# Attention stack kernel: last norms on GpSimd, x-stage logits in pairs, two query windows in one matmul, and another order of work in the slots

## The chip, the cores and the metric

The kernel runs on one core of a Trainium2 chip. Its time is the device time in microseconds (us) of one execution of the whole program; of several runs the median is given. The core's engines run side by side, each in the order of its own instruction stream, and wait for each other through semaphores: PE (TensorE, matrix products, with PEld for its weight loads), DVE (VectorE), ACT (ScalarE), POOL (GpSimd) and SP, which issues the DMAs.

## The reference, cut to what matters

There are 16 sequences of 128 tokens of 128 numbers. First comes one cross-attention layer (the x stage), then six layers, each a local attention and a gated feed-forward.

```python
x = x + tanh(g_xattn[0]) * xattn(layernorm(x), ctx, ctx, fside, ...)   # 16 heads of 8; bias from clip(frac_k - frac_q, -0.2, 0.2)
x = x + tanh(g_ffn[0]) * ffn(layernorm(x), ...)
# ffn:
for i in range(6):
    x = attn_layer(shift_tokens(x), Wqkv[i], ...) + x      # 16 heads of 64
    x = ffn_layer(shift_tokens(x), ln_g[i], ...) + x
# attn_layer: q = l2norm(q) * qs; k = l2norm(k) * ksc; rotary; then windows of 32 queries:
#   queries of window w see the keys of windows w-1 and w, with a band mask, softmax, times v; out @ Wo
# ffn_layer: xn = (x - mean) / sqrt(var + 1e-5) * g + b; (a * gelu(gate)) @ W2 + b2
# shift_tokens: the last 64 features of a token are taken from the token before it
```

## The kernel before, in words

A tile is one sequence (T, with n its number in the layer and par its parity). All state `z` stays on the chip. The order on each engine is written out by hand, in functions named `slot` of the same shape on all engines, and `layer_slots` runs 16 of them a layer: slots 0, 1, 14 and 15 are written out, slots 2 to 13 are a loop over pairs. A slot for tile T carries three tiles at once: it does scores and softmax of T, the projection of T+1 (chunks 0 to 5, of which 0, 1, 3 and 5 are halves of q and k and 2 and 4 are v), and the end of T-1 and T-2 (attention output, residual, LayerNorm statistics).

For a q or k chunk PE projects into one of two banks (`project`, L455 to L457, three matmuls of 512 columns), ACT squares it (L816), DVE multiplies by the rotary tables (`times_cos`, `times_sin`, L1091), sums the squares (L1103) and clamps (L1108), ACT makes the inverse norm by log and exp (`norms`, L820 and L822), POOL adds (`add_rotated`, L1502) and scales (`scale_rotated`, L1509), PE transposes (`qk_transpose`, L465) and ACT copies out. A bank is projected into again only when DVE is done with it (semaphore `rotated`).

For half the heads (h is 0 or 1) of a tile, `scores` (L476) fills `s_ps`, DVE adds the band mask (L1115) and takes row maxima (L1122), POOL subtracts them (`center`, L1515), ACT takes exp, PE transposes, `values` (L506) multiplies by v, DVE inverts the sums and normalises (L1130, L1134), PE transposes the result into `y_ps` (`att_transpose`, L516) and `out_project` (L524) follows. `scores` and `values` are 32 small matmuls each: 4 head pairs, 2 heads of a pair on the upper and lower 64 rows of PE's array (r), 4 windows of 32 queries (w), each writing 32 partitions. Windows 0 and 1 take the same 64 keys (`keys_of`).

The LayerNorm of T-2 in a slot: `add_out` (L1347) adds the residual, PE shifts the second 64 features into `y_ps` (`shift_state`, L529), `ln_stats` on DVE multiplies the first 64 features of `z` by 1.0 into `xs` (L1352), copies the shifted ones from `y_ps` (L1353), and takes the statistics of the 128 (L1355); `ln_variance` (L1359), `ln_std` on ACT (L854, L856) and `ln_apply` on DVE (L1363, into `xn`) follow. `z_stage` (L1298) holds a tile of `z` for the next projection but one. PE's `att_transpose` for half 0 writes `y_ps` again and so waits for `xs_ready`, the mark that both parts of `xs` are there.

The x stage has slots of its own (`x_slot`): for each of four head groups g, `x_scores` on PE adds three matmuls of 512 columns for the bias (L565 to L567, all 128 rows) and one for the logits (L571, on 32 rows, those from 32g) in bank g % 2 of `s_ps`; DVE, ACT and POOL make probabilities, PE transposes (L485) and multiplies by the values (L581).

At a layer's end the feed-forward of the four groups of four tiles runs interleaved with the projection of the next layer's tile 0. There ACT holds the table for gelu, so `ln_std` of the last two tiles takes a table load before and after it (L1036, L1039), and the four `norms` of the next tile stand after the load L1053. POOL makes `f_lo` (`f_rest`, L1611), for which PE's `f_up` (L677 to L679) waits.

## Time and profile before

| | us |
|---|---|
| median of 3 runs | 2065.31 (2059.34 to 2075.24) |
| the profiled execution's own time | 2061.48 |
| its span, first to last instruction | 2059.7 |
| span up to the first scores of layer 1 (x stage and start) | 274.3 |
| one layer, from scores to scores | about 289 |
| a loop slot of a layer | 15.2 to 15.5 |
| a loop slot of the x stage | 13.3 |
| busy: PE, DVE, ACT, POOL | 1797.2, 1600.0, 1384.6, 1332.1 |

The profile is of one execution. The span leaves out 1.8 us of its own time. The granted clock of PE was 0.97 of full speed over the span and 1.00 in the loop slots shown below.

### The profile page before, as it was taken

To read this page: it belongs to the slowest core of one execution; us is meant where nothing else is said; L and a number is where in the kernel's file an instruction comes from. 1 tells how busy PE (TensorE), PEld (TensorE's weight loads), DVE (VectorE), ACT (ScalarE), POOL (GpSimd) and SP (SyncE) were. 2 spreads that over 40 slices of the span, in tenths; PEclk is the share of its full clock that TensorE was granted. 3 is DMA by queue.
4 is the path that set the end of the run, shared out by engine and by line. 5 is a ranking of instruction groups with operands and counts; after the bars stand their busy time and mean duration, and the time that the engine had idled before them with its cause. 6 is when DMAs were issued, how large, how long until landed. Compare 5 with 4: busy or idle time off the path is not lost.

```text
span 2059.7 us, 86637 instructions
## 1 busy us (share of the span) xinstructions
PE 1797.2 (87%) x33584; PEld 1401.8 (68%) x33584; DVE 1600.0 (78%) x3772; ACT 1384.6 (67%) x3701; POOL 1332.1 (65%) x1226
## 2 busy tenths in 40 slices
PE   6999878998879898789988899988898988899887
PEld 3445457777667776677776677776677776677766
DVE  5766679898468987488896589885689885689984
ACT  3677657777557776567775577775577775577765
POOL 3444467777467777377775477774677773677773
PEclk9999979999989999999999999999899999899999
DMA  5000021111021111111110211110211110211111
GB/s 121 4 5 5 1 70 33 35 37 32 25 64 41 31 36 28 63 34 33 40 31 23 68 40 31 41 31 23 64 44 31 31 42 22 65 37 37 31 33 46
DMA packets 59120, 77.81 MB, mean 38 GB/s; under 512 B 16608, under 2 KB 31674, under 8 KB 57914
## 3 DMA queue, kind: packets, MB, share of 16 engines
q1 hardware_dynamic: 58938, 75.36, 13.9%
q8 instruction: 117, 1.92, 0.4%
q14 instruction: 65, 0.53, 0.1%
HBM read 22.63 MB, written 1.05 MB: 11 GB/s over the span
## 4 chain that ended last, share of the span: by engine, by line
PE 60%; DVE 15%; issue 12%; ACT 6%; POOL 5%; SPq 0%; DMA 0%; DVEq 0%; ACTq 0%; POOLq 0%
PE proj_ps L455 7%; PE s_ps L476 7%; PE tr_ps L465 7%; PE y_ps L524 7%; PE proj_ps L457 5%; PE proj_ps L456 5%; PE y_ps L516 4%; DVE by_cos L1091 3%; PE pv_ps L506 3%; ACT square L816 3%; DVE by_sin L1091 3%; DVE xs L1352 3%; PE s_ps L571 3%; DVE sumsq L1103 2%; PE s_ps L691 2%
## 5 line engine op out<-in xcount | busy, mean ns | idle before, releaser
L1502 POOL TENSOR_TENSOR qk<-by_cos,by_sin 128x512 f32<-128x512 f32 x388 | 495.3, 1276 | 208.3 <-DVE by_sin L1091 201.9
L1509 POOL TENSOR_TENSOR qk<-qk,inv_norm 128x512 f32<-128x512 f32 x388 | 404.8, 1045 | 68.7 <-ACT inv_norm L822 41.6
L1091 DVE TENSOR_TENSOR by_cos<-proj_ps,tab 128x512 f32<-128x512 f32 x364 | 249.4, 685 | 159.6 <-ACT square L816 158.6
L816 ACT ACTIVATE square<-proj_ps 128x512 f32<-128x512 f32 x364 | 217.4, 597 | 195.1 <-PE proj_ps L457 194.8
L1515 POOL TENSOR_TENSOR s_sb<-s_sb,row_max 128x512 f32<-128x512 f32 x192 | 202.7, 1056 | 136.1 <-DVE row_max L1122 136.1
L455 PE MATMUL proj_ps<-w_hi,x_hi 128*128 128x512 f32 x546 | 273.8, 502 | 4.8 <-DVE by_sin L1091 2.6
L465 PE MATMUL tr_ps<-ident,qk 128*128 128x128 f32 x1544 | 247.2, 284 | 24.2 <-ACT x_hi L810 11.8
L1103 DVE TENSOR_REDUCE sumsq<-square 128x8 f32<-128x512 f32 x388 | 262.2, 676 | 0.0
L1091 DVE TENSOR_TENSOR by_sin<-proj_ps,tab 128x512 f32<-128x512 f32 x364 | 247.8, 681 | 0.0
L465 PEld LDWEIGHTS tr_ps<-ident,qk 128*128 128x128 f32 x1544 | 184.0, 146 | 72.5 <-POOL qk L1509 28.5
L457 PE MATMUL proj_ps<-w_hi,x_lo 128*128 128x512 f32 x546 | 222.1, 407 | 0.0
L456 PE MATMUL proj_ps<-w_lo,x_hi 128*128 128x512 f32 x546 | 221.6, 406 | 0.0
L516 PE MATMUL y_ps<-ident,att 128*128 128x128 f32 x768 | 117.8, 276 | 102.7 <-DVE xs L1353 102.7
L476 PE MATMUL s_ps<-k_T,q_T 64*32 64x64 f32 x12288 | 168.7, 227 | 36.8 <-issue 34.5
L524 PE MATMUL y_ps<-wo,att_T 128*128 128x128 f32 x1536 | 187.7, 275 | 0.0
L476 PEld LDWEIGHTS s_ps<-k_T,q_T 64*32 64x32 f32 x12288 | 137.2, 107 | 72.3 <-issue 72.3
L524 PEld LDWEIGHTS y_ps<-wo,att_T 128*128 128x128 f32 x1536 | 179.8, 192 | 8.7
L828 ACT ACTIVATE q_T<-tr_ps 128x512 f32<-128x512 f32 x193 | 114.9, 595 | 90.4 <-PE tr_ps L465 90.4
L516 PEld LDWEIGHTS y_ps<-ident,att 128*128 128x128 f32 x768 | 85.8, 141 | 116.3 <-issue 113.2
L506 PE MATMUL pv_ps<-arena,p_T 64*32 64x65 f32 x7680 | 163.7, 226 | 0.0
L506 PEld LDWEIGHTS pv_ps<-v,p_T 64*32 64x32 f32 x4608 | 122.0, 106 | 53.3 <-issue 52.8
L506 PE MATMUL pv_ps<-v,p_T 64*32 64x65 f32 x4608 | 153.3, 225 | 4.8 <-ACT p_T L846 4.8
(172 smaller groups left out, 4167.1 us busy)
## 6 DMA issues: line engine op xcount, KB each, us to landing
arena<-v SPq DMA_DIRECT2D x388, 130.0 KB, 2.4
w_raw<-in_L_ffn_Wqkv SPq DMA_DIRECT2D x7, 1536.0 KB, 7.3
wo<-in_L_ffn_Wo SPq DMA_DIRECT2D x7, 512.0 KB, 3.8
w_raw<-in_L_ffn_W SPq DMA_DIRECT2D x7, 341.0 KB, 5.5
c_in<-in_ctx SPq DMA_DIRECT2D x16, 64.0 KB, 1.8
xn<-in_fside_BxS SPq DMA_DIRECT2D x1, 1024.0 KB, 6.0
out<-z SPq DMA_DIRECT2D x4, 256.0 KB, 3.0
w<-in_L_ffn_W SPq DMA_DIRECT2D x12, 64.0 KB
```

Source lines behind the costliest of these rows:

```text
L455: pe.matmul(ps[:], x_hi[:], w_hi[:, col], start=True, stop=False)
L456: pe.matmul(ps[:], x_hi[:], w_lo[:, col], start=False, stop=False)
L457: pe.matmul(ps[:], x_lo[:], w_hi[:, col], start=False, stop=True).then_inc(proj_full, 1)
L465: mm = pe.transpose(tr_ps[:, 128 * j:128 * j + 128], qk[:, c, 128 * j:128 * j + 128], ident[:])
L476: mm = pe.matmul(s_ps[toks, slot_of(r, w), 64 * a:64 * a + 64], q_T[par][feat, PAIRS * h + a, toks], k_T[par][feat, PAIRS * h + a, keys_of ...
L506: mm = pe.matmul(pv2_ps[toks, r, (DH + 1) * a:(DH + 1) * (a + 1)], p_T[keys, h, a, toks], src[keys, PAIRS * h + a, :], start=True, stop=True)
L516: mm = pe.transpose(y_ps[:, 128 * j:128 * j + 128], att[:, 8 * i + 2 * j:8 * i + 2 * j + 2, :].rearrange("p a b -> p (a b)"), ident[:])
L524: mm = pe.matmul(y_ps[:, 0:D], att_T[:, c, :], wo[:, c, :], start=(c == 0), stop=(c == 7))
L1091: return dve.tensor_tensor(dst[:, c % 2, :].rearrange("p (h d) -> p h d", d=DH), ps, tb, ALU.mult)
L1103: dve.tensor_reduce(sumsq[:, c, :, 0], square[:, c % 2, :].rearrange("p (h d) -> p h d", d=DH), AX, ALU.add).then_inc(summed, 1)
L1502: pool.tensor_tensor(heads(qk[:, c, :]), heads(by_cos[:, c % 2, :]), heads(by_sin[:, c % 2, :])[:, :, ::-1, :], ALU.add).then_inc(qk_added, 1)
L1509: pool.tensor_tensor(ap, ap, inv_norm[:, c, :].unsqueeze(2).to_broadcast([128, 8, DH]), ALU.mult).then_inc(qk_ready, 1)
```

## The change

Six edits, in the core of the diff below.

1. `QUERIES`: in `scores` and `values` the first two windows become one matmul of 64 queries, so 24 matmuls stand where 32 stood, 8 of them of 64 queries and 16 of 32.
2. `ln_stats` no longer copies the first half of `z` into `xs`; statistics are taken of `z` and `xs` apart (two instructions of 64 numbers), and `ln_apply` has two instructions of 64 columns.
3. The orders in `slot` on PE, ACT, DVE and POOL change. On DVE `ln_apply` moves from after group 3 to before it, `z_stage` from before the mask of half 1 to after it, and the row maxima of half 1 come after two products; on PE `shift_state` comes after `project` 1 and `qk_transpose` 3, `att_transpose` 0 after `project` 2.
4. In the x stage `x_scores` handles two head groups: bias of g, logits of g, logits of g+1, bias of g+1.
5. At a layer's end POOL makes the last two deviations (`own_deviations`) and the four inverse norms of the next tile (`own_norm`) by power -0.5; ACT's `ln_std` there and one table load are gone, and one load of the exp table is left.
6. POOL's `scale_rotated` of a chunk at the layer's end follows directly on its `add_rotated`.

```diff
+QUERIES = [(slice(0, 2 * WINDOW), 1), (slice(2 * WINDOW, 3 * WINDOW), 2), (slice(3 * WINDOW, 4 * WINDOW), 3)]
...
@@ PE, scores (values likewise)
-                        for w in range(NT // WINDOW):
-                            feat, toks = slice(64 * r, 64 * r + 64), slice(WINDOW * w, WINDOW * w + WINDOW)
+                        for toks, w in QUERIES:
+                            feat = slice(64 * r, 64 * r + 64)
                             mm = pe.matmul(s_ps[toks, slot_of(r, w), 64 * a:64 * a + 64], q_T[par][feat, PAIRS * h + a, toks],
...
@@ PE, x stage
+            def x_bias(T, par, g, first):
+                hi, lo = flat(pos_hi[:, GH * g:GH * g + GH]), pos_lo[g]
+                pe.matmul(s_ps[:, g % 2, :], d_hi[:, par], hi, start=first, stop=False)
+                pe.matmul(s_ps[:, g % 2, :], d_hi[:, par], lo, start=False, stop=False)
+                return pe.matmul(s_ps[:, g % 2, :], d_lo[:, par], hi, start=False, stop=not first)
+
+            def x_logits(T, par, g, first):
+                rows = slice(32 * g, 32 * g + 32)
+                return pe.matmul(s_ps[:, g % 2, :], xq[rows, par, :], flat(xk_bd[rows, par]), start=first, stop=not first)
...
                 if after(T, 1) or g >= 2:
                     pe.wait_ge(masked, T * 4 + (g - 1))
+                x_bias(T, par, g, True)
                 if g == 0:
                     pe.wait_ge(xk_ready, T + 1)
+                if after(T, 1) or g >= 2:
+                    pe.wait_ge(masked, T * 4 + g)
+                x_logits(T, par, g, False).then_inc(s_full, 1)
+                x_logits(T, par, g + 1, True)
+                x_bias(T, par, g + 1, False).then_inc(s_full, 1)
...
@@ PE, x_slot
-                x_scores(T, par, 1)
...
-                x_scores(T, par, 3)
...
@@ ACT, a layer's end
-                act.preload_act_table_set("natural_log_exp_and_others")
-                ln_std(T - 2, 0)
-                ln_std(T - 1, 1)
-                act.preload_act_table_set("gelu_and_others")
+                act.sem_inc(log_done, 2)
...
@@ DVE
                 def ln_stats(T, n, par):
-                    zt = tile_of(z, n, 0, D // 2)
                     dve.wait_ge(sh_full, T + 1)
-                    dve.tensor_scalar(xs[:, par, 0:D // 2], zt, 1.0, None, ALU.mult).then_inc(xs_ready, 1)
-                    dve.tensor_copy(xs[:, par, D // 2:D], y_ps[:, 0:D // 2]).then_inc(xs_ready, 1)
-                    dve.wait_ge(xs_ready, T * 2 + 2)
-                    dve.bn_stats(stats[:, par], xs[:, par]).then_inc(stat_done, 1)
+                    dve.tensor_copy(xs[:, par], y_ps[:, 0:D // 2]).then_inc(xs_ready, 1)
+                    dve.bn_stats(stats[:, par, 0], tile_of(z, n, 0, D // 2))
+                    dve.wait_ge(xs_ready, T + 1)
+                    dve.bn_stats(stats[:, par, 1], xs[:, par]).then_inc(stat_done, 1)
...
                 def ln_apply(T, n, par):
                     dve.wait_ge(rstd_ready, T + 1)
-                    dve.tensor_scalar(tile_of(xn, n), xs[:, par],
-                                      mean_var[:, par, 0:1], rstd[:, par:par + 1], ALU.subtract, ALU.mult).then_inc(xn_ready, 1)
+                    for lo, src in ((0, tile_of(z, n, 0, D // 2)), (D // 2, xs[:, par])):
+                        last = dve.tensor_scalar(tile_of(xn, n, lo, lo + D // 2), src,
+                                                 mean_var[:, par, 0:1], rstd[:, par:par + 1], ALU.subtract, ALU.mult)
+                    last.then_inc(xn_ready, 1)
...
@@ POOL
+            def own_norm(T, c):
+                pool.wait_ge(norm_ready, T * 4 + (c + 1))
+                pool.tensor_tensor(inv_norm[:, c, :], sumsq_min[:, c, :], minus_half[:], ALU.pow).then_inc(inv_ready, 1)
...
+                def own_deviations(T):
+                    pool.wait_ge(var_ready, T)
+                    pool.tensor_tensor(log_var[:], mean_var[:, :, 1], eps[:].to_broadcast([128, 2]), ALU.add).then_inc(var_added, 1)
+                    pool.wait_ge(var_added, L)
+                    pool.tensor_tensor(rstd[:], log_var[:], minus_half[:, 0:2], ALU.pow).then_inc(rstd_ready, 2)
...
                 split_x(T)
+                own_deviations(T)
                 f_rest(2)
                 add_rotated(T, 0)
                 f_rest(3)
+                own_norm(T, 0)
+                scale_rotated(T, 0)
                 for c in range(1, 4):
                     add_rotated(T, c)
-                first_scales(T)
+                    own_norm(T, c)
+                    scale_rotated(T, c)
+                split_x(T + 1)
```

**PE at the start of a loop slot.** `s_ps<-k_T,q_T` is `scores`, and the size at the end is the output's: partitions by columns. Before:

```order
L470 ISA
L476 MATMUL s_ps<-k_T,q_T 32x64 x32
L445 REGISTER_ALU
L446 ISA
L455 MATMUL proj_ps<-w_hi,x_hi 128x512
L456 MATMUL proj_ps<-w_lo,x_hi 128x512
L457 MATMUL proj_ps<-w_hi,x_lo 128x512
L489 ISA
L490 REGISTER_ALU
L492 MATMUL pv_ps<-ident,p_sb 128x128 x4
```

Now:

```order
L481 MATMUL s_ps<-k_T,q_T 64x64
L481 MATMUL s_ps<-k_T,q_T 32x64 x2
L481 MATMUL s_ps<-k_T,q_T 64x64
L481 MATMUL s_ps<-k_T,q_T 32x64 x2
L450 REGISTER_ALU
L451 ISA
L460 MATMUL proj_ps<-w_hi,x_hi 128x512
L461 MATMUL proj_ps<-w_lo,x_hi 128x512
L462 MATMUL proj_ps<-w_hi,x_lo 128x512
L494 ISA
L495 REGISTER_ALU
L497 MATMUL pv_ps<-ident,p_sb 128x128 x4
```

The 32 equal matmuls became eight times a matmul of 64 queries and two of 32 (the last two of the eight are shown). In `values` it is the same.

**DVE in the second half of a loop slot.** `xn` is the LayerNorm of T-2, `by_cos` to `sumsq_min` the chunks of T+1. Before:

```order
L1103 TENSOR_REDUCE sumsq<-square 128x8
L1108 TENSOR_REDUCE sumsq_min<-sumsq 128x8
L1094 REGISTER_ALU
L1091 TENSOR_TENSOR by_cos<-proj_ps,tab 128x512
L1091 TENSOR_TENSOR by_sin<-proj_ps,tab 128x512
L1103 TENSOR_REDUCE sumsq<-square 128x8
L1130 RECIPROCAL inv_sum<-pv_ps 128x8
L1108 TENSOR_REDUCE sumsq_min<-sumsq 128x8
L1134 TENSOR_TENSOR att<-pv_ps,inv_sum 128x2x4x64
L1363 REGISTER_ALU
L1363 TENSOR_SCALAR xn<-xs,mean_var,rstd 128x128
```

Now:

```order
L1093 TENSOR_TENSOR by_cos<-proj_ps,tab 128x512
L1093 TENSOR_TENSOR by_sin<-proj_ps,tab 128x512
L1124 TENSOR_REDUCE row_max<-s_sb 128x8
L1105 TENSOR_REDUCE sumsq<-square 128x8
L1299 REGISTER_ALU
L1300 ISA
L1300 TENSOR_SCALAR z_stage<-z 128x128
L1110 TENSOR_REDUCE sumsq_min<-sumsq 128x8
L1364 REGISTER_ALU
L1364 TENSOR_SCALAR xn<-z,mean_var,rstd 128x64
L1364 ISA
L1364 TENSOR_SCALAR xn<-xs,mean_var,rstd 128x64
```

`xn` moved from the slot's end to between groups 2 and 3 and is in two parts, and `z_stage` now stands two instructions ahead of it. On POOL the order beside this place is now `add_rotated` 2, `center` 1, `scale_rotated` 2.

**PE in the x stage, one pair of head groups.** `pos_hi` and `f_hi` are the bias, `gelu,xq` the logits. Before:

```order
L565 MATMUL s_ps<-pos_hi,w_hi 128x512
L566 MATMUL s_ps<-f_hi,w_hi 128x512
L567 MATMUL s_ps<-pos_hi,w_lo 128x512
L571 MATMUL s_ps<-gelu,xq 128x512
L481 ISA
L483 REGISTER_ALU
L485 MATMUL pv_ps<-ident,p_sb 128x128 x4
L541 ISA
L542 REGISTER_ALU
L543 MATMUL tr_ps<-ident,arena 128x128
L544 MATMUL tr_ps<-ident,c_in 128x128
L581 MATMUL pv_ps<-p_T,arena 32x128 x4
```

Now:

```order
L578 ISA
L563 MATMUL s_ps<-pos_hi,w_hi 128x512
L564 MATMUL s_ps<-f_hi,w_hi 128x512
L565 MATMUL s_ps<-pos_hi,w_lo 128x512
L569 MATMUL s_ps<-gelu,xq 128x512 x2
L563 MATMUL s_ps<-pos_hi,w_hi 128x512
L564 MATMUL s_ps<-f_hi,w_hi 128x512
L565 MATMUL s_ps<-pos_hi,w_lo 128x512
```

The logits of two groups now follow each other, and the transposes and values that stood between groups g and g+1 come after both.

## Rows read from the trace of the kernel before

**Rows 1.** The page: busy time of the engines, its chain by engine.

```profile
PE 1797.2 (87%) x33584; PEld 1401.8 (68%) x33584; DVE 1600.0 (78%) x3772; ACT 1384.6 (67%) x3701; POOL 1332.1 (65%) x1226
...
PE 60%; DVE 15%; issue 12%; ACT 6%; POOL 5%; SPq 0%; DMA 0%; DVEq 0%; ACTq 0%; POOLq 0%
```

**Rows 2.** Three loop slots, the first and their mean: length, busy us of each engine.

```profile
666.32:681.55 15.23, 13.89 (x333) 11.58 (x341) 13.57 (x31) 11.18 (x30) 11.61 (x12) 1.00 0.14 34
...
sum 45.92, PE 41.74 PEld 34.71 DVE 40.93 ACT 33.88 POOL 35.18; mean PE 13.91 PEld 11.57 DVE 13.64 ACT 11.29 POOL 11.73
```

**Rows 3.** Waits: who waited for whom, us in total, times, longest.

```profile
PE y_ps L516 <- DVE xs L1353: 102.7, 78, 1.4
```

**Rows 4.** The chain in order of time in a loop slot: start, us, what.

```profile
701.60 0.76 DVE xs L1352
```

**Rows 5.** Timeline of a loop slot: start, us, engine, instruction [idle before, releaser].

```profile
685.65 1.27 POOL L1502 TENSOR_TENSOR qk<-by_cos,by_sin 128x512 f32<-128x512 f32 x1 [0.23 <-DVE by_sin L1091]
...
686.21 0.77 DVE L1352 TENSOR_SCALAR xs<-z 128x64 f32 x1
...
686.89 0.21 DVE L1353 COPY xs<-y_ps 128x64 f32<-128x64 f32 x1
...
687.14 0.29 DVE L1355 BATCH_NORM_STATS2 stats<-xs 128x6 f32<-128x128 f32 x1
...
687.25 0.63 PE L516 MATMUL y_ps<-ident,att 128*128 128x128 f32 x4 [1.34 <-DVE xs L1353]
```

**Rows 6.** Single lines: duration ns least/median/most, first and last start.

```profile
L1352 DVE TENSOR_SCALAR xs<-z x96: 143/762/768, 310.5 to 2025.5; 128x64 f32 x72, 128x64 f32<-128x64 f32 x24
...
L1363 DVE TENSOR_SCALAR xn<-xs,mean_var,rstd x96: 335/339/1210, 322.0 to 2031.1; 128x128 f32 x72, 128x128 f32<-128x128 f32 x24
...
L1298 DVE TENSOR_SCALAR z_stage<-z x98: 191/195/730, 251.2 to 2044.7; 128x128 f32 x72, 128x128 f32<-128x128 f32 x26
```

**Rows 7.** Timeline of that slot's second half.

```profile
692.16 0.68 DVE L1091 TENSOR_TENSOR by_sin<-proj_ps,tab 128x512 f32<-128x512 f32 x1
...
693.00 1.28 POOL L1502 TENSOR_TENSOR qk<-by_cos,by_sin 128x512 f32<-128x512 f32 x1 [0.23 <-DVE by_sin L1091]
...
695.12 0.69 DVE L1091 TENSOR_TENSOR by_cos<-proj_ps,tab 128x512 f32<-128x512 f32 x1 [1.49 <-ACT square L816]
```

**Rows 8.** Timeline at the start of a call of scores.

```profile
704.33 0.70 PEld L476 LDWEIGHTS s_ps<-k_T,q_T 64*32 64x32 f32 x64 [0.17 <-issue]
704.33 0.86 PE L476 MATMUL s_ps<-k_T,q_T 64*32 64x64 f32 x64
```

**Rows 9.** An x-stage loop slot: window as in rows 2, PE's timeline.

```profile
114.53:127.84 13.31, 12.75 (x78) 6.58 (x79) 8.80 (x35) 9.87 (x40) 5.23 (x7) 1.00 0.02 5
...
121.19 0.50 PE L565 MATMUL s_ps<-pos_hi,w_hi 128*128 128x512 f32 x1
...
121.53 0.39 PE L566 MATMUL s_ps<-f_lo,w_hi 128*128 128x512 f32 x1
...
121.76 0.40 PE L567 MATMUL s_ps<-pos_hi,w_lo 128*128 128x512 f32 x1
...
122.08 1.12 PE L571 MATMUL s_ps<-gelu,xq 32*128 32x512 f32 x2
...
123.14 0.66 PE L485 MATMUL pv_ps<-ident,p_sb 128*128 128x128 f32 x4
```

**Rows 10.** Timeline of a layer's end.

```profile
839.31 0.45 POOL L1496 TENSOR_TENSOR x_lo<-x_all,x_hi 128x128 fp32r<-128x128 f32 x1 [9.15 <-ACT x_hi L810]
...
840.79 1.27 POOL L1611 TENSOR_TENSOR f_lo<-f_all,f_hi 128x512 fp32r<-128x512 f32 x1 [1.02 <-ACT f_hi L963]
...
842.19 0.50 PE L677 MATMUL proj_ps<-f_hi,w_hi 128*128 128x512 f32 x1 [0.89 <-POOL f_lo L1611]
```

**Rows 11.** Groups by line: busy us, mean ns of one, idle before.

```profile
L1515 POOL TENSOR_TENSOR s_sb<-s_sb,row_max 128x512 f32<-128x512 f32 x192 | 202.7, 1056 | 136.1 <-DVE row_max L1122 136.1
...
L1496 POOL TENSOR_TENSOR x_lo<-x_all,x_hi 128x128 fp32r<-128x128 f32 x98 | 44.7, 456 | 92.4 <-ACT x_hi L810 92.2
```

More of the change, by code:

```diff
@@ L501, in values @@
                     for r in range(2):
-                        for w in range(NT // WINDOW):
-                            i, toks = slot_of(r, w), slice(WINDOW * w, WINDOW * w + WINDOW)
+                        for toks, w in QUERIES:
+                            i = slot_of(r, w)
                             keys = slice(64 * i, 64 * i + 64)
@@ L599, in x_slot @@
                     x_values(T - 1, 1 - par, 1)
-                x_scores(T, par, 1)
-                if not first:
                     x_p_transpose(T - 1, 3)
@@ L705, in slot @@
                         p_transpose(T - 1, 1)
-                    if behind >= 2:
-                        shift_state(T - 2, tile_of(z, n - 2, D // 2))
+                    if front_on:
+                        project(T + 1, 1)
                     if first:
@@ L731, in slot @@
                         qk_transpose(T + 1, 1)
+                        project(T + 1, 5)
                     values(T, par, 0)
-                    if front_on:
-                        project(T + 1, 5)
-                        if not last_front:
-                            x_transpose(T + 2)
+                    if front_on and not last_front:
+                        x_transpose(T + 2)
                     if behind >= 1:
@@ L928, in first_out @@
             def first_out(T):
-                for c in range(4):
-                    norms(T, c)
+                act.sem_inc(inv_log, 4)
                 x_out(T + 1)
@@ L1395, in slot @@
                         add_out(T - 2, n - 2)
-                    step(T, 0, behind, front_on)
-                    if behind >= 2:
-                        ln_stats(T - 2, n - 2, par)
+                    mask(T, 0)
+                    row_maxima(T, 0)
                     if not front_on:
@@ L1403, in slot @@
+                    if behind >= 1:
+                        sums_inverse(T - 1, 1)
+                    if behind >= 2:
+                        dve.wait_ge(stat_done, T - 1)
+                    if behind >= 1:
+                        normalise(T - 1, 1)
                     if behind >= 2:
                         ln_variance(T - 2, par)
+                    if front_on:
+                        clamp_norm(T + 1, 1)
+                    mask(T, 1)
+                    if not front_on:
+                        w_round(1, L + 1)
@@ L1590, in slot @@
                         pool.tensor_tensor(w1_lo[:], w1_raw[:], w1_hi[:].bitcast(f32), ALU.subtract).then_inc(w1_split, 1)
-                    for g in range(NG):
-                        if g == 0:
-                            if not first:
-                                scale_rotated(T, 3)
-                        elif front_on:
-                            scale_rotated(T + 1, g - 1)
-                        if g % 2 == 0:
-                            center(T, g // 2)
-                        if not front_on and 1 <= g < 3:
-                            w_rest(g - 1, L * 3 + g)
-                        if front_on:
-                            if g == 3 and not last_front:
-                                split_x(T + 2)
-                            add_rotated(T + 1, g)
-                layer_slots(pool.Fori, L, slot)
+                    if not first:
+                        scale_rotated(T, 3)
+                    center(T, 0)
+                    if not front_on:
+                        w_rest(0, L * 3 + 1)
+                    if front_on:
+                        add_rotated(T + 1, 0)
+                        scale_rotated(T + 1, 0)
+                        add_rotated(T + 1, 1)
+                        scale_rotated(T + 1, 1)
+                        add_rotated(T + 1, 2)
+                    center(T, 1)
+                    if not front_on:
+                        w_rest(1, L * 3 + 2)
+                    if front_on:
+                        scale_rotated(T + 1, 2)
+                    if front_on and not last_front:
+                        split_x(T + 2)
+                    if front_on:
+                        add_rotated(T + 1, 3)
+                layer_slots(pool.Fori, L, slot)
+                def own_deviations(T):
[3 more added lines that the diff above has]
+                    pool.tensor_tensor(rstd[:], log_var[:], minus_half[:, 0:2], ALU.pow).then_inc(rstd_ready, 2)
                 def f_rest(j):
```

129 lines of the change are left out of this document (63 added, 66 removed).

## Prediction

> **What bounds the kernel now.** I read the page first, then the windows of the loop slots, then the waits, the chain and the timeline. The page gives PE 87% of the span and 60% of the chain, DVE 78% and 15% [rows 1]. A share over the whole span doesn't say what an edit is worth, so I take the loop slot of a layer, which makes up most of the time. Three such slots are 45.92 us together, 15.31 us each; PE is busy for 13.91 us of a slot, DVE for 13.64, POOL for 11.73, ACT for 11.29 [rows 2]. PE's missing 1.4 us is nearly one wait: att_transpose waits for DVE's xs, 102.7 us over 78 slots, 1.32 us each [rows 3]. The chain confirms that it is on the path: it leaves PE, goes over DVE's products and sums to xs at L1352, and comes back to PE [rows 4]. The timeline shows what this step is: L1352 takes 0.77 us there and ends at 686.98, just after POOL's addition has ended at 686.92 [rows 5]. Its least duration is 143 ns, its median 762 [rows 6]. So about 0.6 us of it is a wait for POOL's instruction, and in that form the same can hit L1363 (335 ns least, 1210 most) and z_stage (191, 730) [rows 6]. DVE is nearly as full as PE: beside small gaps it idles 1.49 us in a slot, once, before the cosine product of group 3 [rows 7].
>
> The Trainium skill, page SBUF — State Buffer, section Who interferes with whom, has the shared port pair of VectorE and GpSimd as an exclusive lock, held for a whole instruction by whichever started first. By that rule, the trace agrees: 0.77 us against 0.14 [rows 5, 6].
>
> **The loop slots, part by part.** PE: with the wait gone a slot can't be shorter than PE's own work, about 13.9 us. The merged windows take a quarter of the matmuls out of four calls. A call is about 0.8 us (704.33 to 705.12 in the chain, 0.86 with the modelled end [rows 8]); the bounds are no gain, if the time goes by columns streamed per row and column of the array, and a quarter of it, 0.2 us, if it goes by instructions, so 0 to 0.8 us a slot. I take 0.2, since POOL and DVE will hide what goes beyond that, and keep the bounds for the range.
>
> DVE: from 13.64 us the xs instruction goes, at most 0.76, of which the copy after it overlapped a little: minus 0.70 [rows 4, 5]. One more statistics instruction of 64 numbers costs up to the 0.29 of the present one of 128 [rows 5]: plus 0.2. The xn instruction of 128 columns takes 0.34 [rows 6]; two halves cost the fixed part twice: plus 0.2. That gives 13.35 us, if nothing waits for POOL.
>
> But three of these DVE instructions now stand where POOL is busy. Before, add_rotated 2 started 0.84 us after the start of its sine product (692.16 to 693.00) and took 1.28, so it ended 2.1 us after that start [rows 7]. In the new order DVE does sine product 2, row maxima, sum of squares 2 and then z_stage, at three times 0.6 us = 1.8 us after the sine product's start. It meets the addition and waits 0.3 us. The clamp follows, and xn would start some 0.2 us later, at 2.3. POOL's next is center 1, whose row maxima have long been there; it starts about 0.1 us after the addition's end, at 2.2, and takes 1.06 [rows 11]. So the first half of xn comes 0.1 us too late and waits about 0.9 us. The second half then races scale_rotated 2; I let it win. DVE's slot is 13.35 + 0.3 + 0.9 = 14.55 us. PE needs 13.7, POOL and ACT less, and the wait for square 3 is covered by DVE's own lateness. I take 14.5 us: 0.8 us less than 15.3. Over the 78 slots that show the wait this is 62 us. For the 18 others, which begin or end a layer, I take nothing, for want of a steady pace.
>
> The other moves of order on PE, ACT and POOL cost nothing in this sum: their cover is the slack of PE, 14.5 against 13.7. Were DVE quicker, they would count, since PE's project 2 then waits for the sine product of group 0, which ends about when PE gets there.
>
> **The x stage.** PE is busy 12.75 of 13.31 us of a slot, so it is the bound [rows 9]. A group takes 1.95 us (121.19 to 123.14): bias to 122.08, logits 1.06 [rows 9]. Among equal shapes a matmul of 512 columns follows at 0.23 us (121.53, 121.76), but the logits, on 32 rows, start 0.32 us after the last bias [rows 9]: a change of shape has a price of about 0.1 us, and twice a pair is one change saved. If the logits of two groups, on different 32 rows, overlap as the 64-row halves of scores do (64 records in 0.86 us where one lasts over 0.2 [rows 8]), a pair saves the 1.06 of one and some of the changes, 1.3 us, so 2.6 a slot. PE would drop to about 10.5, and DVE (8.80 busy) and ACT (9.87 busy) [rows 9] are next; and the pair's second logits must wait for the mask of the group before. I take 2.0 us a slot, 14 slots, 28 us. If nothing overlaps, only the changes are saved, 0.4 us a slot, 6 us.
>
> **The layer's end.** Two table loads and four small ACT instructions leave ACT, and POOL gets ten small ones. PE is the bound there, working through the feed-forward; what can touch it is POOL's f_lo, for which PE waited 0.89 us [rows 10]. Before this f_lo POOL was idle 1.02 us [rows 10], and there own_deviations now stands, two instructions with a wait between. No row shows a power on POOL. The cheapest POOL row is 0.456 us for 128 columns, against 1.06 for 512 [rows 11], so 8 numbers should be nearer 0.3: two fit into 1.02. Were each 1.3 us, as long as a whole addition, PE would wait 1.8 us more, 11 us over six layers. A gain is bounded by the 0.89 us wait times six, 5 us. The inverse norms lie in POOL's long idle stretches. I take 0.
>
> **The sum.** The profiled execution took 2061.48 us, of which the span is 2059.7. 2061.5 - 62 - 28 = 1971.5. The median of the runs shown is 3.8 us above this execution; I give **1972 us**.
>
> **The rivals.** First, slower: the array drains. In scores and values, matmuls for 64 and for 32 queries now alternate, 16 changes a call. Where the shape changes today, PE's weight loads stand idle 0.17 us, though nothing was late [rows 8], and in the x stage too the follow-on is late [rows 9]. At 0.17 us a change a call gets 16 x 0.17 = 2.7 us longer, and 96 tiles x 4 calls = 384 calls make 1045 us: 1972 + 1045, about 3015 us. It decides from 90 / 384 = 0.23 us a call on, that is with two changes of sixteen that drain. For it: every change of shape in the trace shows the wait. Against it: in all of those the new shape takes rows and columns that the old one occupies, whereas here 64 queries write partitions 0 to 63 and the others 64 to 127, always the same parts, so nothing needs to be cleared.
>
> The Trainium skill, page TensorEngine Tiling (Array Packing), section Key Properties, states this rival's rule: changing the tiling mode, not just the tile, drains the TensorE. Its page TensorE: Matmul & The Clock Gate, section Part 3, has the position carried by each instruction, with tiles overlapping, which speaks for the forecast. No row here has two disjoint shapes in turn.
>
> Second, the port race is lost twice: the second half of xn finds scale_rotated 2 running, plus 1.05 us a slot. The slot is 15.5 us, the loop slots gain nothing, and only the x stage is left: about 2035 us, or 2025 if DVE's lateness shifts POOL a little. DVE's whole idle time of 1.5 us is then used up.
>
> Third, the race is won and the merging pays in full: DVE 13.4, PE 13.9 - 0.8 = 13.1, a slot of about 13.6. That is 1.7 x 78 = 133 and 28 off: about 1900 us.
>
> Fourth, the change doesn't do what it says in the x stage, no overlap of logits: the forecast plus 22, 1994 us.
>
> **How the numbers follow.** Forecast 0.35, and with the fourth case (0.09) in its surroundings 1940 to 2000; second case 0.22; third 0.15; drain 0.17; 0.02 for other mishaps above 2060. Leaving out the drain and the mishaps is 0.19, so the range goes from 1895 (third case) to 2045 (second with its spread). No change here means within 1%, 20.7 us, about what a measurement can tell. Faster: 0.35 + 0.09 + 0.15 + most of the second = 0.78. Same 0.05. Slower 0.17.
>
> **What the profile after would show.** Right: the wait of att_transpose for xs gone; loop slots of about 14.5 us with DVE busy over 14; xn's first half with a median near 1.2 us, its second near 0.3; z_stage near 0.5. A call of scores between 0.6 and 0.85 us; if over 1, the array drains. x slots of 11.3 us. POOL's powers under 0.5 us. I would be wrong mostly by the alternating shapes, whose price no row shows, and by the race for the port, where 0.1 us decides about 1 us a slot.

## The result and the profile after

| | before | after |
|---|---|---|
| median | 2064.48 us (2059.34 to 2075.24) | 3461.26 us (3455.89 to 3464.95) |
| ratio | | 1.675, 95% interval 1.668 to 1.682 |
| span of the profiled execution | 2059.7 us | 3460.0 us |
| granted clock of PE over the span | 0.97 | 0.85 |
| loop slot of a layer, mean | 15.3 us | 30.0 us |
| a call of scores | 0.8 us | 3.9 us |

The forecast was 1972 us. The rival that the array drains, with 3015 us and a chance of 0.17, is what happened, and it too was priced low. One of the four executions of w4_sin, a kernel below, took 2663 us at a granted clock of 0.56; its interval leaves it out.

The page of the kernel after: busy time, the granted clock in tenths by slices, the chain by engine, and one of the costliest groups (`s_sb<-s_ps` is the first step of DVE behind `scores`).

```profile
PE 3319.4 (96%) x27440; PEld 2425.7 (70%) x27440; DVE 1666.7 (48%) x3869; ACT 1376.0 (40%) x3617; POOL 1364.7 (39%) x1262
...
PEclk9987888877888888898888888888888887888888
...
PE 83%; issue 10%; POOL 3%; DVE 2%; ACT 1%; SPq 0%; DMA 0%; POOLq 0%; DVEq 0%; ACTq 0%
...
L1117 DVE TENSOR_TENSOR s_sb<-s_ps,band 128x512 f32<-128x512 f32 x192 | 132.8, 692 | 925.0 <-PE s_ps L481 925.0
```

DVE, ACT and POOL do the work of before in nearly the same busy time [rows 1]; PE's went from 1797 to 3319 us with 6144 records fewer. DVE now waits for `scores` 192 times, 925 us together. What a call costs is read from the chain in order of time, here inside one slot (start, us, what):

```profile
1206.27 3.90 PE s_ps L481 x48
1210.17 0.46 PE proj_ps L460
1210.63 0.43 PE proj_ps L461
1211.05 0.43 PE proj_ps L462
```

The call takes 3.90 us where the same row of before's chain had 0.79 (x53 are the records that this chain passes, of 64):

```profile
704.40 0.79 PE s_ps L476 x53
```

The inside of the call, by windows whose edges are set where the size changes (us, PE busy and its count, PEld busy and its count, clock):

```profile
1206.19:1206.44 0.25, 0.24 (x2) 0.19 (x2) 1.00 0.00 0
1206.44:1206.68 0.24, 0.24 (x6) 0.14 (x4) 1.00 0.00 0
1206.68:1206.93 0.25, 0.25 (x6) 0.19 (x2) 1.00 0.00 0
1206.93:1207.17 0.24, 0.24 (x6) 0.14 (x4) 1.00 0.00 0
```

PEld's counts tell it: two weight loads (the two passes of one matmul of 64 queries), then four (two matmuls of 32 queries), then two, then four. A block of one size takes 0.24 us, whether it holds one matmul or two. Sixteen blocks are 3.9 us. What stands between two blocks shows at the first change (start, us, x2 are the two passes, started at 1206.20 and 1206.31):

```profile
1206.20 0.33 PE L481 MATMUL s_ps<-k_T,q_T 64*64 64x64 f32 x2
...
1206.45 0.10 PEld L481 LDWEIGHTS s_ps<-k_T,q_T 64*32 64x32 f32 x1
```

The first weight load of the other size starts 0.15 us after the start of the last matmul of the old one, just before its modelled end of 1206.53. Within one size the next load starts long before that. The clock stands at 1.00 in this stretch, so it isn't the cause; it comes on top, after the call:

```profile
1208.00:1210.00 2.00, 2.00 (x28) 1.36 (x28) 0.00 (x0) 0.00 (x0) 0.00 (x0) 1.00 0.00 0
1210.00:1212.00 2.00, 2.00 (x11) 1.57 (x10) 0.69 (x1) 0.48 (x1) 0.00 (x0) 0.61 0.00 0
1212.00:1214.00 2.00, 2.00 (x11) 2.00 (x10) 1.85 (x4) 1.71 (x6) 1.41 (x2) 0.54 0.00 0
1214.00:1216.00 2.00, 2.00 (x13) 1.38 (x11) 2.00 (x6) 1.41 (x5) 1.88 (x2) 1.00 0.00 0
```

Behind two calls, of values and of scores, the granted clock falls from 1.00 to about half, the lower level of 1.2 GHz, for some 3.5 us, and in that time matmuls of 512 columns follow each other at 0.43 us in place of 0.23 (the chain above). How much of that falls into a slot varies; this is one of the fastest (length, then PE's busy time, the clock behind POOL's):

```profile
1206.27:1234.04 27.77, 27.77 (x262) 20.79 (x263) 14.45 (x32) 11.61 (x30) 11.65 (x11) 0.94 0.08 20
```

### The profile page after: what moved, and what is told of

It is laid out like the page before. It is cut to its first block, busy times and chain, and to the rows that moved or that the text cites. A ratio compares the mean times of both kernels' runs of the same rounds, so it can differ in the third digit from the quotient of the medians.

```text
span 3460.0 us, 74388 instructions
## 1 busy us (share of the span) xinstructions
PE 3319.4 (96%) x27440; PEld 2425.7 (70%) x27440; DVE 1666.7 (48%) x3869; ACT 1376.0 (40%) x3617; POOL 1364.7 (39%) x1262
## 3 DMA queue, kind: packets, MB, share of 16 engines
q8 instruction: 101, 1.65, 0.2%
HBM read 22.63 MB, written 1.05 MB: 7 GB/s over the span
## 4 chain that ended last, share of the span: by engine, by line
PE 83%; issue 10%; POOL 3%; DVE 2%; ACT 1%; SPq 0%; DMA 0%; POOLq 0%; DVEq 0%; ACTq 0%
PE s_ps L481 23%; PE pv_ps L511 20%; PE proj_ps L460 7%; PE tr_ps L470 6%; PE proj_ps L461 5%; PE proj_ps L462 5%; PE y_ps L529 5%; PE y_ps L521 3%; PE pv_ps L497 3%; PE s_ps L703 1%; POOL w_lo L1504 1%; PE s_ps L569 1%; POOL p_sb L1538 1%; PE tr_ps L444 1%; POOL f_lo L1631 1%
## 5 line engine op out<-in xcount | busy, mean ns | idle before, releaser
L481 PE MATMUL s_ps<-k_T,q_T 64*32 64x64 f32 (+1 forms) x9216 | 864.4, 255 | 22.3 <-issue 19.3
L481 PEld LDWEIGHTS s_ps<-k_T,q_T 64*32 64x32 f32 (+1 forms) x9216 | 556.6, 124 | 332.0 <-issue 114.2
L511 PE MATMUL pv_ps<-arena,p_T 64*32 64x65 f32 (+1 forms) x6144 | 630.2, 238 | 0.0
L1117 DVE TENSOR_TENSOR s_sb<-s_ps,band 128x512 f32<-128x512 f32 x192 | 132.8, 692 | 925.0 <-PE s_ps L481 925.0
L511 PEld LDWEIGHTS pv_ps<-arena,p_T 64*32 64x32 f32 (+1 forms) x6144 | 364.7, 114 | 184.7 <-issue 6.7
L511 PE MATMUL pv_ps<-v,p_T 64*64 64x65 f32 (+1 forms) x3072 | 442.2, 241 | 9.3 <-ACT p_T L853 9.3
L511 PEld LDWEIGHTS pv_ps<-v,p_T 64*64 64x64 f32 (+1 forms) x3072 | 253.6, 121 | 108.6 <-issue 50.2
L460 PE MATMUL proj_ps<-w_hi,x_hi 128*128 128x512 f32 x546 | 323.6, 593 | 4.7 <-DVE by_sin L1093 2.6
L470 PEld LDWEIGHTS tr_ps<-ident,qk 128*128 128x128 f32 x1544 | 240.5, 172 | 79.6 <-issue 43.1
L857 ACT ACTIVATE att_T<-y_ps 128x512 f32<-128x512 f32 x192 | 114.7, 597 | 438.3 <-PE y_ps L521 437.9
```

The source lines that it names most:

```text
L460: pe.matmul(ps[:], x_hi[:], w_hi[:, col], start=True, stop=False)
L470: mm = pe.transpose(tr_ps[:, 128 * j:128 * j + 128], qk[:, c, 128 * j:128 * j + 128], ident[:])
L481: mm = pe.matmul(s_ps[toks, slot_of(r, w), 64 * a:64 * a + 64], q_T[par][feat, PAIRS * h + a, toks], k_T[par][feat, PAIRS * h + a, keys_of ...
L511: mm = pe.matmul(pv2_ps[toks, r, (DH + 1) * a:(DH + 1) * (a + 1)], p_T[keys, h, a, toks], src[keys, PAIRS * h + a, :], start=True, stop=True)
```

## The experiments

The theory after this reading: PE pays at every change of size, and all of the loss is there. Four kernels test it, on one chip (kernel before there: 2062.6 us).

**Four equal windows (w4).** The kernel after, with the first edit undone.

```diff
-QUERIES = [(slice(0, 2 * WINDOW), 1), (slice(2 * WINDOW, 3 * WINDOW), 2), (slice(3 * WINDOW, 4 * WINDOW), 3)]
+QUERIES = [(slice(WINDOW * w, WINDOW * w + WINDOW), w) for w in range(NT // WINDOW)]
```

> The kernel after, with one part undone: scores and values again have four matmuls for 32 queries each per head, all of one shape; everything else of the change stays. Theory (the alternation of 64 and 32 queries makes PE empty itself at each change; all that was lost was lost there): a call falls from 3.9 us to about 0.9, no wait stands at each change, the clock returns to 0.97 or so, and the time is that of the rest of the change by itself, 1900 to 2045 us. Rival (the new orders in the slots, the GpSimd powers or the pairs of logits cost something as well, hidden under the array's loss now): over 2080 us. Rival (merging as such is harmless and the other edits are the cause): stays above 3000 us. Of the forecast's loop slot this also shows the rest: DVE bound at about 14.5 us if the first half of xn waits for center 1, 15.5 if both halves wait, 13.9 or less if none does; an x slot of 11.3 us if logits on different rows overlap, about 13 if not.

Measured: 1968.45 us (1958.53 to 1976.34), 0.953 of before, interval 0.948 to 0.957. So the five other edits gain 94 us, and the first one costs 1493. Its slots and, for later, two x slots (columns as in [rows 2]):

```profile
698.93:713.33 14.40, 13.96 (x333) 11.50 (x339) 13.98 (x33) 11.50 (x31) 11.78 (x12) 1.00 0.15 37
...
113.65:126.42 12.77, 10.49 (x82) 6.16 (x78) 9.29 (x36) 9.88 (x41) 5.63 (x6) 1.00 0.02 5
126.42:139.53 13.11, 10.74 (x82) 6.24 (x78) 9.18 (x36) 9.77 (x41) 5.62 (x6) 1.00 0.02 5
```

**Merging alone (b_merge).** The kernel before with only `QUERIES` and its two loops.

> The kernel before, with the merged windows as the one edit, alternating as in the kernel after. Theory: 384 calls at 3.9 us in place of 0.86, 1170 us, and the clock falls from 0.97 to about 0.85, which adds some 100 to 250 us to PE's other work: 3250 to 3550 us. Rival (an interplay with the new order on PE is needed): under 2800 us. Rival (merging is not the cause): about 2065 us.

Measured, one run: 3511.31 us, clock 0.84, calls of 3.92 us at full clock and 4.2 where it falls during a call. The interplay with the new order is out: the first edit does it alone, and costs 1449 us there.

**One change inside a call (grouped), seven (halfchg).** The same 24 matmuls per call, ordered otherwise.

```diff
+PLACES = [(a, r, toks, w) for part in (QUERIES[:1], QUERIES[1:]) for a in range(4) for r in range(2) for toks, w in part]   # grouped
+PLACES = [(a, r, toks, w) for a in range(4) for part in (QUERIES[:1], QUERIES[1:]) for r in range(2) for toks, w in part]   # halfchg
...
-                for a in range(PAIRS):
-                    for r in range(2):
-                        for toks, w in QUERIES:
+                for a, r, toks, w in PLACES:
```

> The kernel after, with the same 24 matmuls per call in another order: first the eight of 64 queries, then the sixteen of 32. One change inside a call in place of fifteen. Theory (each change costs about 0.14 to 0.15 us beside its matmuls, whichever parts of the array are written): a call goes from 3.9 us to about 0.8 to 1.1, and the whole to what the kernel with four equal windows takes, within 60 us of it. Rival (a matmul of 64 queries is slow by itself, on this array or in its write to 64 partitions): a call stays above 2 us and the time above 2700 us. Rival (the granted clock fell for another reason and slows all): calls get short but the time stays above 2600 us.

> The kernel after, the same 24 matmuls per call ordered by head pair: the two of 64 queries, then the four of 32. Seven changes inside a call in place of fifteen. Theory (a price per change): a call of about 0.9 + 7 x 0.2 = 2.3 us at most, half of the loss of 3 us; the time 2500 to 2800 us. Rival (a price per matmul of 64 queries): a call stays at 3.9 us and the time near 3461 us. Rival (a price paid once per call): the same as with one change per call.

Measured: grouped 2072.45 us (ratio 1.005, interval 1.003 to 1.007), halfchg 2415.6 us in one run, less than the 2500 to 2800 expected, with a call inside the 2.3 us given for it. The call of scores in their chains, grouped first:

```profile
700.89 1.19 PE s_ps L480 x48
```

```profile
701.77 2.03 PE s_ps L480 x48
```

With 2, 8 and 16 blocks of one size a call takes 1.19, 2.03 and 3.90 us. From 8 to 16 a block costs (3.90 - 2.03) / 8 = 0.23 us, from 2 to 8 (2.03 - 1.19) / 6 = 0.14: a block has a least time of about 0.24 us, and one that holds more work hides part of it. A price per matmul of 64 queries is out, for their number is the same in all three. The clock was 0.975 in grouped and 0.964 in halfchg: it stayed up with calls of 2 us and fell only with calls of 3.9.

One thing went against me: grouped is 104 us slower than w4, more than the 60 allowed. Its call is 0.40 us longer than 0.79, though eight matmuls fewer and with one change. In windows, the first half of the call is the 64-query part and the pause at its end, the second the 32-query part:

```profile
700.81:701.40 0.59, 0.58 (x16) 0.54 (x16) 1.00 0.00 0
701.40:702.00 0.60, 0.60 (x36) 0.49 (x32) 1.00 0.00 0
```

Sixteen records need as long as the other thirty-two. In a part only some of the array's places get work: the 64-query matmuls all sit on output partitions 0 to 63, the 32-query ones on 64 to 127. That led to the next kernel.

**Two sizes or two places (all64).** Windows 2 and 3 in one matmul as well, with the keys of window 3; the keys of window 2 are left out.

```diff
+QUERIES = [(slice(0, 2 * WINDOW), 1), (slice(2 * WINDOW, 4 * WINDOW), 3)]
```

> The kernel after with two matmuls per head and pair, both for 64 queries (windows 0 and 1 with the keys of window 1, windows 2 and 3 with the keys of window 3), so one shape throughout, its place alternating between the output's partitions 0 to 63 and 64 to 127. It leaves out the keys of window 2, so its output isn't the reference's. Theory (a change of size costs, a change of place doesn't): no wait inside a call; 32 matmul records at 0.029 us, a call of about 1.1 us, a slot of 15.3 us, the whole 2040 to 2080 us, clock 0.96 or more. Rival (a change of place between halves costs as well): over 2 us a call and over 2400 us. Rival (fewer matmuls are faster once the shape is one): a call under 0.79 us, the whole under 1968 us.

Measured, one run: 1904.26 us, clock 0.973. The call is over in 0.63 us, 32 records, the next matmul (L460) at 603.54:

```profile
602.91 0.69 PE L481 MATMUL s_ps<-k_T,q_T 64*64 64x64 f32 x32
603.54 0.50 PE L460 MATMUL proj_ps<-w_hi,x_hi 128*128 128x512 f32 x1
```

A change of place between the halves costs nothing; my figure of 1.1 us was wrong and the rival, fewer matmuls are faster once the shape is one, was right. Four matmuls of 64 by 64, on four different places, go side by side. So the price is on the size, and a part that leaves half of the places empty wastes them: in grouped the 64-query part has the places of two.

**The forecast's second half: what sets the slot of 14.40 us?** I had said DVE, which waits for POOL in xn. Four edits of w4 and one of before test that.

**A later xn (w4_late).**

```diff
-                    if behind >= 2:
-                        ln_apply(T - 2, n - 2, par)
                     if front_on:
                         times_cos(T + 1, 3, L - 1)
                         sum_squares(T + 1, 3)
+                    if behind >= 2:
+                        ln_apply(T - 2, n - 2, par)
+                    if front_on:
                         times_sin(T + 1, 3, L - 1)
```

> The kernel with four equal windows and the rest of the change, with one step moved: on DVE xn of T-2 (two instructions) comes between the sum of squares 3 and the sine product 3, and not before the cosine product 3. There POOL has only the short x_lo (0.46 us) or nothing, where it had center 1 (1.05 us) before. Theory (the first half of xn, 0.97 us median, waits about 0.67 us for center 1, and DVE sets the slot of 14.40 us): the first half falls to about 0.3 to 0.6 us, DVE needs 13.7 to 13.9, and PE with 13.96 us busy a slot becomes the bound: slot 13.9 to 14.1, the whole 1925 to 1945 us. Rival (the wait hides in DVE's slack, or POOL's shifted add_rotated 3 gives it back): slot 14.4, 1968 us within 6. Rival (the race goes to z_stage and scale_rotated 2): something between, with z_stage over 0.4 us.

Measured: 1965.06 us (1956.28 to 1973.81), as w4, so the first rival and not the theory. The duration of xn's first half (least/median/most) in w4 and in w4_late:

```profile
L1364 DVE TENSOR_SCALAR xn<-z,mean_var,rstd x96: 301/968/1185, 308.9 to 1943.4; - x72, 128x64 f32<-128x64 f32 x24
```

```profile
L1364 DVE TENSOR_SCALAR xn<-z,mean_var,rstd x96: 301/342/648, 308.3 to 1941.4; - x72, 128x64 f32<-128x64 f32 x24
```

The wait for the port went, DVE's busy time of a slot fell from 13.98 to 13.54, and the slot stayed at 14.4: DVE was not the bound. The chain of w4 says what was; this is its first way out of PE in a slot:

```profile
699.72 0.43 PE proj_ps L460
700.15 0.23 PE proj_ps L461
700.38 0.25 PE proj_ps L462
700.68 0.05 issue
700.73 0.61 ACT square L823
701.40 0.04 issue
701.45 0.69 DVE by_cos L1093
702.14 0.59 DVE sumsq L1105
702.73 0.61 DVE by_sin L1093
703.38 0.51 PE proj_ps L460
```

PE projects chunk 0, ACT squares it, DVE takes cosine, sum and sine product, and only then may PE project chunk 2, 0.24 us late. The new order had put the sum, 0.59 us, between the two products. Once more in the slot the chain leaves PE, over the inverse norm on ACT and POOL's `scale_rotated` to `qk_transpose`. The two waits of PE in w4 (us in total, times, longest):

```profile
PE tr_ps L470 <- POOL qk L1521: 27.0, 97, 1.3
PE proj_ps L460 <- DVE by_sin L1093: 23.1, 87, 0.7
```

PE's own 13.96 us and these two, 0.2 to 0.3 us each, fill the slot of 14.40.

**The sine product first (w4_sin), and both (w4_late_sin).**

```diff
                         times_cos(T + 1, 0, L - 1)
-                        sum_squares(T + 1, 0)
                         times_sin(T + 1, 0, L - 1)
+                        sum_squares(T + 1, 0)
```

> The kernel with four equal windows and the rest of the change, with one swap on DVE: for group 0 the sine product comes before the sum of squares, as in the kernel before, and not after it. Theory (the slot of 14.40 us is a chain through PE: scores, project 0, ACT's square 0, DVE's cosine product, sum and sine product 0, then project 2, which waits 0.2 us; DVE's fullness is not the bound, since freeing 0.4 us there changed nothing): project 2 no longer waits, and the slot goes towards PE's own 13.97 us, 14.0 to 14.2, unless DVE with its wait for the port (13.9 busy) now binds: 1935 to 1955 us. Rival (the wait of qk_transpose for scale_rotated, 0.2 us, takes the whole over, or the later clamp 0 delays a norm): 14.4, 1968 us within 6.

> The same swap, and xn between the sum of squares 3 and the sine product 3. Theory (with PE's chain shortened DVE's wait for the port becomes the next bound): faster than the swap alone by 5 to 20 us, 1925 to 1940 us. Rival (PE's own work binds already with the swap): equal to the swap alone within 5 us. Together with the two runs that have one of the edits or none, this shows whether the port wait ever was on the path.

Measured: w4_sin 1992.74 us (ratio to before 0.966, interval 0.963 to 0.969), mean slot 14.80; w4_late_sin 1951.87 us (0.946, 0.943 to 0.949), mean slot 14.32 (over slots 1 to 14 of all layers, as w4's 14.43). The swap alone is 24 us slower, outside both expectations, and its trace tells why (xn's second half; the first has a median of 967 ns, as in w4):

```profile
L1364 DVE TENSOR_SCALAR xn<-xs,mean_var,rstd x96: 302/1084/2416, 308.0 to 1959.8; 128x64 f32 x72, 128x64 f32<-128x64 f32 x24
```

Now the second half loses too. In w4 POOL had to wait 0.27 us for the inverse norm 2 before `scale_rotated` 2, and xn's second half got in; in w4_sin POOL goes on at once, 0.02 us ahead of it (POOL's row; xn's second half starts at 627.22):

```profile
627.20 1.05 POOL L1521 TENSOR_TENSOR qk<-qk,inv_norm 128x512 f32<-128x512 f32 x1
```

The chain of this slot runs through DVE alone, and DVE's filled slot is the bound. With xn moved away from there, the swap gives a gain: 13 us against w4_late, 0.1 us a slot; the 1925 to 1940 us expected of w4_late_sin were missed. The wait for the sine product has nearly gone there, and PE is busy for 14.20 of 14.33 us (columns as in [rows 2]):

```profile
630.94:645.27 14.33, 14.20 (x333) 11.42 (x340) 13.73 (x36) 11.70 (x31) 11.99 (x12) 1.00 0.15 37
```

The chain still leaves PE in this slot for some 6 us over ACT and DVE, so both are near their limit. The waits for the port, then, were worth nothing in w4, and in w4_sin 0.5 us a slot (14.80 - 14.32). But the two aren't the same wait: w4_sin has the 0.78 us of the second half on top of the 0.67 of the first. What the first alone would cost with the swap was not measured.

**The second edit alone (b_ln).** The kernel before with the new `ln_stats` and `ln_apply`, old order.

```diff
-                    dve.tensor_scalar(xs[:, par, 0:D // 2], zt, 1.0, None, ALU.mult).then_inc(xs_ready, 1)
-                    dve.tensor_copy(xs[:, par, D // 2:D], y_ps[:, 0:D // 2]).then_inc(xs_ready, 1)
+                    dve.tensor_copy(xs[:, par], y_ps[:, 0:D // 2]).then_inc(xs_ready, 1)
+                    dve.bn_stats(stats[:, par, 0], tile_of(z, n, 0, D // 2))
...
+                    for lo, src in ((0, tile_of(z, n, 0, D // 2)), (D // 2, xs[:, par])):
```

> The kernel before with the second edit alone: no copy of z's first half into xs, statistics and xn in two instructions each, old order. Theory (0.6 to 0.7 us of the 1.3 us for which att_transpose waits is the multiplication by 1.0 waiting for GpSimd): the wait falls to 0.6 to 0.8 us, the slot from 15.3 to 14.7, the whole to 2005 to 2025 us. Rival (the wait for the port only moves to the next DVE instruction that needs it, or DVE is so full that the slot stays): 2050 to 2070 us, and the new orders made the gain of the kernel with four windows. Rival (the second xn instruction costs a wait of its own at the slot's end): over 2070 us.

Measured: 2111.13 us, 1.0245 of before (1.0228 to 1.0262), mean slot 15.9, as in the second rival and not the theory. The wait and xn's second half:

```profile
PE y_ps L516 <- DVE xs L1351: 79.5, 78, 1.2
```

```profile
L1363 DVE TENSOR_SCALAR xn<-xs,mean_var,rstd x96: 302/1090/2348, 320.8 to 2077.5; 128x64 f32 x72, 128x64 f32<-128x64 f32 x24
```

`att_transpose` waits 1.02 us in place of 1.32, but the split xn at the slot's end has a second half that meets POOL, and `add_out` behind it is 0.8 us late, which `shift_state` and so `xs` wait for. The edit is a loss by itself. With the new order beside it, in w4, the slots are shorter; the order without this edit was not run.

**The layer's end undone (w4_act), and all together (best).** Edits 5 and 6 taken back in w4; best is that with the later xn and the swap.

```diff
+                act.preload_act_table_set("natural_log_exp_and_others")
+                ln_std(T - 2, 0)
+                ln_std(T - 1, 1)
+                act.preload_act_table_set("gelu_and_others")
...
-                    own_norm(T, c)
```

> The kernel with four equal windows and the rest of the change, with the layer's end undone: ScalarE makes the last two deviations and four inverse norms by log and exp, with the two table loads, and GpSimd has no power; its scale_rotated come after the last add_rotated. Theory (both fit into idle stretches; f_lo comes 1.02 us after x_lo in both traces): 1968 us within 10. Rival (the power of 8 numbers takes 1.65 us on GpSimd, four in a row before the next layer's first scores, and delays them): 15 to 35 us faster than with the powers. Rival (the table loads were on the path): 10 to 20 us slower.

> The swap, the later xn, four equal windows, and the last norms and deviations again on ScalarE. Theory (the layer's end was 1.5 us shorter with ScalarE, six times): 5 to 12 us less than with the powers, 1918 to 1935 us, the fastest of all that give the reference's output. Rival (the difference between 1968 and 1959 was scatter): equal to the same kernel with the powers.

Measured: w4_act 1959.47 us (1959.17 to 1962.55) against 1968.45 (1958.53 to 1976.34) of w4, which ran at another time; best 1950.71 us (0.945 of before, 0.943 to 0.948) against 1951.87 with the powers. The intervals of the first two against before (0.9494 to 0.9526 and 0.9484 to 0.9571) overlap, and of the second pair, run side by side, the difference is 1 us; a cost of the powers is not shown. The 1918 to 1935 us expected of best were missed, and its rival, scatter, fits. The powers fit where I had put them (timeline of POOL at a layer's end in w4), `f_lo` starting 1.02 us after `x_lo`'s end as before [rows 10]:

```profile
517.08 0.46 POOL L1508 TENSOR_TENSOR x_lo<-x_all,x_hi 128x128 fp32r<-128x128 f32 x1 [9.16 <-ACT x_hi L817]
517.50 0.20 POOL L1624 TENSOR_TENSOR log_var<-mean_var,eps 128x2 f32<-128x2 f32 x1
517.84 0.71 POOL L1626 TENSOR_TENSOR rstd<-log_var,minus_half 128x2 f32<-128x2 f32 x1
518.56 1.26 POOL L1631 TENSOR_TENSOR f_lo<-f_all,f_hi 128x512 fp32r<-128x512 f32 x1
```

## Why the prediction was wrong

**The step that failed** is the price of merging in the sum of the loop slot: "I take 0.2" as a gain, with nothing for the changes of size. They were put at nothing in the first rival, because "here 64 queries write partitions 0 to 63 and the others 64 to 127, always the same parts, so nothing needs to be cleared". Measured, a call went from 0.79 to 3.90 us, which is 12.4 us more a slot. w4 and b_merge put this on the merging alone, and the calls of 1.19, 2.03 and 3.90 us with 2, 8 and 16 blocks show that disjoint parts don't help: each change of size makes the next work wait. all64 shows the reverse, other places with one size, free of charge. The Trainium skill, page TensorEngine Tiling (Array Packing), section Key Properties, says that changing the tiling mode, not just the tile, drains the TensorE. By that rule, the runs agree: 0.63 us for a call with the tile alone changing, 3.90 with the mode.

The evidence stood in the trace of before. At its changes from one size to another the new size's first weight load starts 0.14 us after the start of the last matmul of the old size where that one has 64 columns, 0.20 where it has 128, and 0.32 where it has 512 on all rows (medians), each time 0.07 us before that matmul's modelled end, where nothing else is late. The longer that matmul, the later the load, so its end is what is waited for; the changes inside the calls of after, on disjoint parts, have the same 0.14 to 0.15. The prediction's "every change of shape in the trace shows the wait" goes too far, though: from 128 rows to 86, and from 85 columns to 128, there is none. Here the step from L679 to L516 is 0.23 us, as among equal matmuls of 512 columns, and from L457 to the smaller L506 it is 0.33:

```profile
828.28 0.39 PE L679 MATMUL proj_ps<-f_hi,w_lo 128*85 128x512 f32 x1
828.51 0.60 PE L516 MATMUL y_ps<-ident,att 128*128 128x128 f32 x4
```

```profile
700.11 0.40 PE L457 MATMUL proj_ps<-w_hi,x_lo 128*128 128x512 f32 x1
700.44 0.25 PE L506 MATMUL pv_ps<-v,p_T 64*32 64x65 f32 x2
```

All changes that wait are between whole, half and quarter parts of the array (128, 64, 32 rows or columns). I set a reason that no row showed against one that all these rows kept, and gave the drain a chance of 0.17.

**The rival's size.** It had 0.17 us a change, 2.7 a call, on top of a call of 0.8, so 3.5. Measured are 3.9, sixteen blocks of 0.24: about 0.1 us between the starts of a block's two passes and 0.14 to 0.15 to the next size's first load. That is 384 x 3.11 = 1194 us against 1045. And it had no clock: from w4's span, 1974.2 us, to 3460.0 are 1486 us, of which 1194 are the calls. The rest, 292 us, I put down to the lower clock, without a run of its own: the mean loop slot is 30.0 us, and even the fastest of 27.7, which is 0.9 longer than 14.4 + 4 x 3.11, has a stretch at half clock; (30.0 - 26.8) x some 90 slots = 288 us, the same difference seen by slots.

**The gain from merging**, "a quarter of it, 0.2 us": the bound should have gone below nothing, without any drain. In grouped a call is 0.40 us longer, of which the pause is only a part.

**The rest of the forecast came out near, by luck.** For everything but the first edit it says about 1972, and w4 is 1968. But two errors cancel: of 28 us in the x stage 6 came, and of 62 us in the layers 79 (w4's span is 85.5 us shorter than before's). Point by point:

- The loop slot: 14.5 said, 14.40 found. xn's first half: "a median near 1.2", 0.97; its second near 0.3, 0.30; z_stage near 0.5, 0.42. The place of each wait was right. But "DVE's slot is 14.55" as the bound was not, as w4_late shows: the bound is PE's own work with its two waits, for the sine product of `project` 0 and for `scale_rotated`. I had named the first ("ends about when PE gets there") and costed it at nothing. The 14.40 is therefore no success of the working. The gain was 0.9 us a slot, and it came also in slots for which I took nothing.
- The second rival, the port race lost twice, is real: w4_sin loses it, by 0.02 us, and w4 doesn't. That "0.1 us decides about 1 us a slot" was fair; the 0.8 us went to DVE, of which 0.4 reached the slot.
- The wait of `att_transpose` for `xs` is gone in w4. The new statistics alone don't do it, for b_ln keeps 1.02 of 1.32 us.
- The x stage: "I take 2.0 us a slot, 28 us". The logits do overlap, and PE's busy time fell to 10.5 us as said, but the slot went only from 13.3 to 12.8 to 13.1. The first scores of layer 1 start at 268.3 us in place of 274.5: 6 us, the value that I had given for no overlap, though the logits do overlap. In the nine other kernels with this edit it is 264.7 to 269.6, so the gain is 5 to 10 us. Two new waits of PE, once and twice in a slot, took the rest:

```profile
120.06 0.49 PE L604 MATMUL y_ps<-arena,x_att_T 128*128 128x128 f32 x2 [0.96 <-ACT x_att_T L902]
...
121.18 1.13 PE L569 MATMUL s_ps<-gelu,xq 32*128 32x512 f32 x4
...
124.81 0.66 PE L490 MATMUL pv_ps<-ident,p_sb 128*128 128x128 f32 x4 [0.60 <-POOL p_sb L1538]
```

  Two groups' logits now take 1.13 us, as one's did [rows 9]. The probabilities and the attention output come no earlier for it.
- The layer's end: 0 said; nothing beyond a few us found. "POOL's powers under 0.5 us" was wrong: 1.65 us for 8 numbers and 0.71 for 2, hidden in idle time.

## What to carry to other kernels

Before mixing two sizes of small matmuls, count the blocks of one size in a row, not the matmuls: price each block at its least time, and see how many of the array's places each leaves empty. When a wait shows in all rows of one kind, demand a row for an exception before you price it at nothing. A wait that a run removes without moving the time was beside a longer chain; read it again when that chain is cut, for it may then count, or have grown.

## What the runs showed of the hardware

- A block of matmuls of one size inside a mixed sequence took 0.24 us at the least at full clock, with one matmul in it or two; in a uniform sequence 64 records go in 0.79 us, and 32 of 64 by 64 in 0.63.
- At a change between whole, half and quarter parts of the array, disjoint or not, the next weight load starts 0.07 us before the modelled end of the last matmul: 0.14 us after its start with 64 columns, 0.32 with 512. From 128 rows to 86 there is no wait.
- The granted clock fell to 1.2 GHz after calls of 3.9 us full of pauses between sizes, though the profile shows PE as busy throughout (2.00 of 2.00 us). With calls of 2.0 us it was 0.96 over the span, as with none.
- A power on GpSimd: 1.65 us for 128 by 8 numbers, 0.71 for 128 by 2, while a subtraction of 128 by 512 takes 1.05.
- Which short DVE instruction meets POOL's can turn on a swap of two instructions elsewhere in the slot: xn's second half has a median of 0.30 us in w4 and 1.08 in w4_sin.
